# A decoder layer's first score stage: two score buffers instead of one, and the weights' low parts on another engine

## The reference, cut to what matters

```
x = layernorm(x + attn(x))        # linear attention, 16 heads of 16, causal, rms-normed values, output projection
x = layernorm(x + conv_mix(x))    # products of channel pairs with a context, long convolution, skip term
x = layernorm(x + ffn(x))         # gated network, width 2048, weights packed in 4-bit codes with scales
```

## Time and profile before

| | |
|---|---|
| three runs | 579.39 to 581.28 us, median 580.69 us |
| the profiled execution | 580.05 us, of which the span 578.4 us |
| TensorE matmul busy | 524.9 us (91% of the span) |
| VectorE busy | 375.6 us (65%), 782 instructions |
| ScalarE busy | 148.2 us (26%) |
| GpSimd busy | 123.5 us (21%), 195 instructions |
| granted TensorE clock, mean | 0.944 of full speed |

### The profile page before, as it was taken

The page is one execution under the profiler, slowest core; times in us unless marked ns, Lnnn a source line. Parts: engine busy times, 40 slices in busy tenths (PEclk is TensorE's granted clock), DMA queues, the critical chain, the costliest instruction groups (busy, mean ns, idle before and its releaser), DMA issues.

```text
span 578.4 us, 9097 instructions
## 1 busy us (share of the span) xinstructions
PE 524.9 (91%) x3280; PEld 428.4 (74%) x3280; DVE 375.6 (65%) x782; ACT 148.2 (26%) x259; POOL 123.5 (21%) x195
## 2 busy tenths in 40 slices
PE   5855569989989999999999999999999998599993
PEld 5722457776778888876788888776888887488883
DVE  3899659976768566886355577875455768733234
ACT  3422210153243211242232112232232110122220
POOL 2100038420001445030002445120003443200001
PEclk9965569999999999999999999999999999699998
DMA  5523214130020111005000110031001110100001
GB/s 164 160 79 73 71 53 132 56 95 16 21 72 23 43 37 47 0 29 156 1 1 28 47 47 28 0 88 57 0 0 44 47 54 1 37 1 0 1 1 37
DMA packets 25249, 26.69 MB, mean 46 GB/s; under 512 B 2816, under 2 KB 22784, under 8 KB 25216
## 3 DMA queue, kind: packets, MB, share of 16 engines
q1 hardware_dynamic: 14208, 15.73, 9.4%
q10 hardware_dynamic: 10576, 8.95, 5.2%
q0 software_dynamic: 432, 1.57, 0.8%
HBM read 24.15 MB, written 2.10 MB: 45 GB/s over the span
## 4 chain that ended last, share of the span: by engine, by line
PE 81%; DVE 11%; issue 3%; DMA 3%; POOL 1%; ACT 1%; ACTq 0%; POOLq 0%; DVEq 0%; SPq 0%
PE bank L903 16%; PE bank L905 15%; PE bank L904 15%; PE front_bank L1015 5%; PE front_bank L1018 4%; PE front_bank L1016 4%; PE front_bank L964 4%; PE front_bank L951 4%; PE front_bank L992 3%; PE front_bank L903 2%; PE front_bank L904 2%; PE front_bank L905 2%; DVE gate_q L676 2%; PE front_bank L974 1%; DMA wo_sb<-in_woT 1%
## 5 line engine op out<-in xcount | busy, mean ns | idle before, releaser
L903 PE MATMUL bank<-x2T_lo,ffn_hi 128*128 128x512 f32 x256 | 111.1, 434 | 4.1 <-DVE x2T_lo L838 4.1
L854 DVE TENSOR_TENSOR inter<-bank,inter 128x512 f32<-128x512 f32 x64 | 44.2, 690 | 94.3 <-PE bank L905 94.0
L905 PE MATMUL bank<-x2T_hi,ffn_hi 128*128 128x512 f32 x256 | 101.8, 397 | 0.0
L904 PE MATMUL bank<-x2T_hi,ffn_lo 128*128 128x512 f32 x256 | 101.4, 396 | 0.0
L436 POOL TENSOR_TENSOR qbd<-qT_sb,ctxT_sb 128x256 f32<-128x256 f32 x128 | 77.8, 631 | 77.5 <-PE front_bank L1018 63.8
L386 POOL TENSOR_TENSOR ve<-ve,minus_half 128x2 f32<-128x2 f32 x24 | 17.4, 743 | 305.5 <-DVE ve L726 235.4
L903 PE MATMUL bank<-ffn_lo,inter_hi 128*128 128x256 f32 x256 | 77.2, 302 | 0.8 <-DVE inter_lo L848 0.8
L588 ACT ACTIVATE inter_hi<-inter 128x512 fp32r<-128x512 f32 x64 | 40.5, 632 | 141.9 <-DVE inter L854 141.9
L582 ACT ACTIVATE inter<-bank 128x512 f32<-128x512 f32 x64 | 38.2, 598 | 134.3 <-PE bank L905 134.2
L905 PE MATMUL bank<-ffn_hi,inter_hi 128*128 128x256 f32 x256 | 72.0, 281 | 0.0
L904 PE MATMUL bank<-ffn_hi,inter_lo 128*128 128x256 f32 x256 | 71.9, 281 | 0.0
(11 more groups left out here) (113 smaller groups left out, 768.9 us busy)
## 6 DMA issues: line engine op xcount, KB each, us to landing
toep_sb<-in_toep ACTq DMA_DIRECT2D x64, 128.0 KB, 2.1
xT_sb<-in_xT SPq DMA_DIRECT2D x4, 512.0 KB, 6.1
ctxT_sb<-in_ctxT SPq DMA_DIRECT2D x4, 512.0 KB, 4.7
x_sb<-in_x SPq DMA_DIRECT2D x4, 512.0 KB, 5.7
ctx_sb<-in_ctx SPq DMA_DIRECT2D x4, 512.0 KB, 6.8
out<-ctxT_sb POOLq DMA_DIRECT2D x3, 512.0 KB, 3.4
raw_w<-in_gate_p SPq DMA_DIRECT2D x8, 128.0 KB
raw_s<-in_gate_s SPq DMA_DIRECT2D x8, 128.0 KB
```

Source lines behind the costliest of these rows:

```text
L854: nc.vector.tensor_tensor(inter[:, n % 2, :], up_ps[:, :], inter[:, n % 2, :], ALU.mult).then_inc(inter_ready, 1)
L903: nc.tensor.matmul(ps, w_hi, x_lo, start=start, stop=False, skip_group_check=True)
L904: nc.tensor.matmul(ps, w_lo, x_hi, start=False, stop=False, skip_group_check=True)
L905: return nc.tensor.matmul(ps, w_hi, x_hi, start=False, stop=stop, skip_group_check=True)
```

## The change

In the first group alone (`alone(g)`), odd score steps put their raw scores into the gated network's banks, now one tensor `ffn_ps` (`ffn_bank`), and their masked scores into `inter` (`odd_sc_sb`). TensorE's `score` there issues the raw scores of step u ahead of the values of step u-1; for u from 2 on they wait until mask step u-2 is done. VectorE's mask step waits for the values of step u-1 when u is even and of step u-2 when it is odd. And the low parts of all 24 units are computed by GpSimd, unit n directly after its high part, in place of VectorE two units later. In `turn`, GpSimd's first spread moves behind the first of its four pieces. The other groups' score steps keep their order.

```diff
+        odd_sc_sb = inter[:].rearrange("p n (h c) -> p (n h) c", c=P)
...
-        psum = [None] * 4 + [stack.enter_context(nc.psum_tensor(f"bank{i}", [P, T], F32)) for i in range(4, 8)]
+        ffn_ps = stack.enter_context(nc.psum_tensor("ffn_bank", [P, 4, T], F32))
...
+        def scores_ps(g, u):
+            return ffn_ps if alone(g) and u % 2 else front_ps
+        def masked_scores(g, u):
+            return odd_sc_sb if alone(g) and u % 2 else sc_sb
...
@@ GpSimd
+            def unpack(step):
+                n = step - 1
+                if 0 <= n < NU:
+                    m, c = units[n]
+                    pool.wait_ge(whi_ready, n + 1)
+                    nc.gpsimd.tensor_tensor(ffn_lo[:, m, :, c * QC:(c + 1) * QC], weight[:, n % 2],
+                                            ffn_hi[:, m, :, c * QC:(c + 1) * QC].bitcast(F32), ALU.subtract)\
+                        .then_inc(wlo_ready, 1)
...
                 if g is not None:
-                    for pair in range(4):
+                    beside(0)
+                    spread(g, 1)
+                    for pair in range(1, 4):
                         beside(pair)
-                    spread(g, 1)
...
@@ VectorE
-                q = n - 2
-                if 0 <= q < NU:
-                    m, c = units[q]
-                    dve.wait_ge(whi_ready, q + 1)
-                    nc.vector.tensor_tensor(ffn_lo[:, m, :, c * QC:(c + 1) * QC], weight[:, q % 2],
-                                            ffn_hi[:, m, :, c * QC:(c + 1) * QC].bitcast(F32), ALU.subtract)\
-                        .then_inc(wlo_ready, 1)
...
-                count(dve, o_mm, NU_S, g, u)
-                nc.vector.tensor_tensor(sc_sb.rearrange("p (r k) c -> p r k c", k=2),
-                                        front_ps[:, :, 0:2 * P].rearrange("p r (k c) -> p r k c", c=P),
+                count(dve, o_mm, NU_S, g, u - u % 2 if alone(g) else u)
+                nc.vector.tensor_tensor(masked_scores(g, u).rearrange("p (r k) c -> p r k c", k=2),
+                                        scores_ps(g, u)[:, :, 0:2 * P].rearrange("p r (k c) -> p r k c", c=P),
...
@@ TensorE
+            def raw_scores(g, u):
...
+                if alone(g) and u >= 2:
+                    count(pe, sm_ready, NU_S, g, u - 1)
...
             def score(g, u):
+                if alone(g):
+                    if u < NU_S:
+                        raw_scores(g, u)
+                    if u:
+                        values(g, u - 1)
+                else:
+                    if u:
+                        values(g, u - 1)
+                    if u < NU_S:
+                        raw_scores(g, u)
```

More of the change, by code:

```diff
@@ L140, in by_seq, with alone @@
             return tile[:, mt, :].rearrange("p (b t) -> p b t", t=S)
-        gate_ps, up_ps = psum[4], psum[5]
-        down_ps = psum[6:8]
-        skip_ps = x2T_ps = psum[4:6]
+        gate_ps, up_ps = ffn_ps[:, 0, :], ffn_ps[:, 1, :]
+        down_ps = [ffn_ps[:, i, :] for i in (2, 3)]
+        skip_ps = x2T_ps = [gate_ps, up_ps]
+        def alone(g):
+            return isinstance(g, int) and g == 0
+        def scores_ps(g, u):
+            return ffn_ps if alone(g) and u % 2 else front_ps
+        def masked_scores(g, u):
+            return odd_sc_sb if alone(g) and u % 2 else sc_sb
         def sems(*names):
@@ L449, in turn @@
                     pool.dma_start(out_v[:, bass.ds(at, NB), :], res_sb).then_inc(stored, 16)
-            schedule(pool, turn, {"score": score, "norm": norm, "x1T": x1T, "conv": conv}, nothing, nothing, nothing, nothing,
+            schedule(pool, turn, {"score": score, "norm": norm, "x1T": x1T, "conv": conv}, nothing, nothing, nothing, unpack,
                      lambda: rstd(G - 1, 2))
@@ L573, in turn @@
                         count(act, x2T_mm, 2, prev, w + 1)
[L574 removed]
+                        nc.scalar.activation(x2T_hi[:, w, :], x2T_ps[w], ACT.Copy).then_inc(x2hi_ready, 1)
                 if g is not None:
@@ L775, in x2_half @@
                 count(dve, skip_mm, 2, g, j + 1)
-                nc.vector.tensor_tensor(ctx2, skip_ps[j][:, :], ctx2, ALU.mult).then_inc(sk_ready, 1)
+                nc.vector.tensor_tensor(ctx2, skip_ps[j], ctx2, ALU.mult).then_inc(sk_ready, 1)
                 count(dve, cT_mm, 2, g, j + 1)
@@ L861, in finish @@
                     dve.wait_ge(last_mm, j + 1)
-                    nc.vector.tensor_tensor(res_sb[:, pair].rearrange("p b f -> p (b f)"), down_ps[j][:, :],
+                    nc.vector.tensor_tensor(res_sb[:, pair].rearrange("p b f -> p (b f)"), down_ps[j],
                                             x2_sb[:, pair].rearrange("p b f -> p (b f)"), ALU.add)\
@@ L938, in vproj @@
                 last.then_inc(v_mm, 1)
-            def score(g, u):
[L943 to L967, removed]
@@ new lines, in values @@
+            def values(g, v):
+                mt, b = v // NB, v % NB
+                if v == 0:
+                    count(pe, v_ready, 2, g, 2)
+                count(pe, sm_ready, NU_S, g, v + 1)
+                for odd in range(2):
+                    for pair in range(4):
+                        last = nc.tensor.matmul(
+                            front_ps[32 * pair:32 * pair + 32, b, 256 + mt * S:256 + (mt + 1) * S],
+                            v_sb[:, b, 4 * mt + pair, DK * odd:DK * odd + 2 * DK],
+                            masked_scores(g, v)[:, 2 * pair + odd, :], start=odd == 0, stop=odd == 1)
+                last.then_inc(o_mm, 1)
@@ new lines, in raw_scores @@
+            def raw_scores(g, u):
+                mt, b = u // NB, u % NB
+                if u == 0:
+                    count(pe, qk_ready, 4, g, 4)
+                    count(pe, v_ready, 2, g, 2)
+                if alone(g) and u >= 2:
+                    count(pe, sm_ready, NU_S, g, u - 1)
+                count(pe, spread_ready[u % 2], NU_S // 2, g, u // 2 + 1)
+                for r in range(4):
+                    rows = slice(32 * r, 32 * r + 32)
+                    last = nc.tensor.matmul(scores_ps(g, u)[:, r, 0:2 * P].rearrange("p (k c) -> p k c", c=P),
+                                            kT_sb[rows, mt, b * S:(b + 1) * S], q_two[rows, u % 4, 0:2],
+                                            start=True, stop=True)
+                last.then_inc(s_mm, 1)
```

10 lines of the change are left out of this document (5 added, 5 removed).

## The result

| | before | after |
|---|---|---|
| median of 12 runs each | 579.97 us (579.39 to 581.75) | 586.62 us (583.3 to 587.66) |
| ratio, 95% interval | | 1.0104 (1.0088 to 1.012) |
| the profiled execution; its span | 580.05; 578.4 us | 587.31; 585.7 us |
| VectorE busy | 375.6 us, 782 instructions | 379.7 us, 758 instructions |
| GpSimd busy | 123.5 us, 195 | 153.2 us, 219 |

The account below looks back on a forecast made before the run. A three-engine ring set the 3.59 us score step; breaking it would be waited away behind GpSimd's subtractions (3.66). Terms 0.8 + 2.2 + 0.7 + 0.3 + 0.5 = +4.5 on 580.05, plus 0.64 to the median: 585.2 us, range 581.5 to 588.5.

Parts of the forecast that it names:

- the rival of the races: Transposes, second `turn` and slot 6 at their low ends, first mask step at +0.2: +1.6, 582.2 us; chance 0.10.
- Start of the stage, +0.8: Up to the first mask step: GpSimd's subtractions delay unit 1 and meet pieces 2 and 4; +0.8 us, between -0.5 and +1.2.
- Score steps, +2.2: First group's steps 0 to 7: 3.66 us each plus 1.4 for three spreads, 27.0 against 24.84 us: +2.2.
- First layer norm, +0.7: Unit 15's subtraction delays the third and fourth normalisations and the last two transposes: +0.7 us, between 0 and +1.1.
- Second `turn`, +0.3: Unit 17's subtraction races the fourth normalisation: +0.9 - 0.48, or about -0.3 if the subtraction comes behind; taken as +0.3 us.
- Slot 6, +0.5: First group's back half: the subtraction starts beside VectorE's piece while TensorE idles; +1.0 - 0.48 gives +0.5 us, at best -0.5.
- The other slots: Other subtractions priced at nothing, lying where VectorE or GpSimd waits for TensorE; without that cover each could cost 0.5 us.
- The rival "no exclusion": GpSimd's subtraction does not keep VectorE out: step 2.79 us, -6.3 us in all, 574.4 us; chance 0.08.
- Slower GpSimd, 588: Rounding to float32r and two separate stretches make the subtraction 0.3 us slower in some ten places: 588 us; chance 0.12.
- An early release: The lock is let go after 0.47 us: score step 3.0 us, -2.4, the rest about even, 578.2 us; chance 0.06.

Follow-up runs that it names:

- e2: The changed kernel without its score part: one score buffer in the old order, low parts still on GpSimd; 586.40 us.
- e5: The changed kernel, but from piece 18 on (second `turn`, slots) GpSimd's subtraction also waits until VectorE's piece there is done; 582.65 us.
- e6: The changed kernel, but GpSimd subtracts unit 15 ahead of the first layer norm's powers instead of behind them; 585.64 us.
- e1: The changed kernel without its GpSimd part: two score buffers, low parts on VectorE again; 578.47 us.
- e3: The changed kernel with the first twelve pieces' and piece-18-on subtractions waiting for VectorE, unit 15 before the first layer norm's powers, unit 16 behind the second's normalisations; 575.24 us.
- e7: The changed kernel, but in the first twelve pieces GpSimd's subtraction also waits until VectorE's next unit is done; 580.87 us.
- e9: The kernel with all subtractions moved, and the first group's odd spreads on ScalarE instead of GpSimd; 574.63 us.
- e8: The changed kernel with each GpSimd subtraction replaced by a memset of zeros of the same size; 575.93 us.

## Why the prediction was right, and where it was not

The forecast, 585.2 us and slower, lies 1.4 us below the measured 586.62. That it lies so near is in part luck: it stood on 580.69, the median of three runs, where twelve give 579.97, so that the change cost 6.65 us and the forecast of +4.5 is 2.15 short. (One small slip: the rival of the races comes to 580.69 + 1.6 = 582.3, not 582.2.) Its reason held: GpSimd's subtraction and the instructions of VectorE that the sum named, shifts, bit mask, product and normalisations, exclude each other for their whole length. The mark that it gave for them, to read and write SBUF alone, is too wide, as the last section shows. The row on which it rested, and that no trace of before had, is the pair of 42.77: it waits until 43.72 for an instruction of 512 columns. The Trainium skill, "SBUF — State Buffer", section "Who interferes with whom", has the lock held for the full instruction; the trace agrees for the subtraction, with 1.27 us. Step by step:

- **Start of the stage, +0.8:** +0.84, beside a -0.56 of earlier transfers that has nothing to do with the change (that event lies at 13.56 to 14.72 us in the ten traces). The prediction had pieces 2 and 4 meet a subtraction. All of pieces 1 to 4 did, and idle time took up the rest; the size is right, the account of it too small. The size also holds beyond the one trace: it is 16.04 to 16.38 us in the four kernels with this front (after, e2, e5, e6), and 15.30 and 15.54 in the two without the subtractions (e1, before).
- **Score steps, +2.2:** +1.75. A step is 3.62, not 3.66, since the subtraction starts 0.74 us behind a piece's end (38.41 - 37.67) and not 0.79; a spread behind it costs 0.42 (1.73 - 1.31), not 0.47, three times.
- **First layer norm, +0.7:** +0.83. The third and fourth normalisations waited for unit 15's subtraction. e6 took it away and got 0.77 back at that place. The 0.31 us in the convolution were not in the sum: TensorE's clock was 0.50 from 86 to 92 us, where it was 0.95 before. Whether they belong to the change is not shown: e1, without the subtractions, takes 27.54 us for that stretch, as against 27.27 before and 27.58 after.
- **Second `turn`, +0.3:** +0.63. The prediction left open which side wins the race, and took a value between. The subtraction won, twice. VectorE, then GpSimd of the kernel after, in order of time:

```profile
124.99 1.58 DVE L671 SCALAR_TENSOR_TENSOR weight<-code,raw_s 128x512 f32<-128x512 f16 x1
126.50 2.33 DVE L754 TENSOR_SCALAR x_sb<-x_sb,mv,ve 128x256 f32<-128x256 f32 x4
...
124.56 1.47 POOL L457 TENSOR_TENSOR ffn_lo<-weight,ffn_hi 128x512 fp32r<-128x512 f32 x1
127.32 1.36 POOL L457 TENSOR_TENSOR ffn_lo<-weight,ffn_hi 128x512 fp32r<-128x512 f32 x1 [1.29 <-ACT ffn_hi L510]
```

  Unit 16's subtraction holds up the product with the scales (1.58 us), unit 17's the normalisations (2.33 instead of 1.37). The prediction had seen the second one alone.
- **Slot 6, +0.5:** +0.64, as described, by a subtraction that started 0.02 us ahead of the shifts.
- **What was missing:** the +1.56 behind slot 6, a term that the sum had at nothing without a reason. The prediction priced TensorE's longer idle time at its length and stopped there; it did not ask what the clock does behind a longer gap. e5 shows both go together: without the gap neither is there. The other slots were rightly priced at nothing (0 and -0.21 us over their stretches).

The five terms of the sum came to 4.7 us where 4.5 stood. What moves the time beyond it is the clock: behind slot 6 by the longer gap (e5), at the convolution (0.31) and at the end of the kernel (1.42 us of the profiled run) without a cause that a run shows. The rival "no exclusion", 574.4 us, is refuted as a mechanism, and its time came true another way: e3, in which the exclusion is there but falls mostly on work that it does not touch, takes 575.24. Slower GpSimd, 588, did not happen where the two did not meet: 1.27 us, as the earlier trace rows, so rounding to float32r costs it nothing. An early release is refuted by the stretched pair.

Two things stay open. Two of the twelve runs of the changed kernel took 583.3 and 583.5 us at a mean clock of 0.944 to 0.947, and the others 585.4 to 587.7 at 0.934 to 0.940; which stretch of low clock those two were spared no trace shows. Where slot 6 has the same gap, other kernels have such runs too (one of four of e2 at 583.1, three of ten of e7 at 577.6 to 578.8 against 580.5 to 582.5), so it is not shown that the 1.56 us, seen in four traces of four, falls due in every run. And nothing was tried against the transfer that ends the wait in e9.

## What to carry to other kernels

Work handed from VectorE to GpSimd was free here while VectorE waited or ran its mask step, which has an input in PSUM; over the shifts, masks, products and normalisations, which read and write SBUF alone, it cost VectorE GpSimd's longer time (1.27 us here) for VectorE's shorter one (0.69). So look not at how idle GpSimd is, but at which of VectorE's instructions its own will fall on, and put it there by a wait: a few added waits for a later event made the same instructions 1% faster than before instead of 1% slower. And where TensorE idles already, price a longer gap by the clock behind it as well.

## What the runs showed of the hardware that was not expected

- An instruction of GpSimd that reads nothing holds VectorE's shifts too: the zeros of e8, until 40.23, against a pair that starts at 40.03 and takes 0.54 us instead of 0.48; of the overlap the first 0.14 us cost nothing, as in the other pairs here (0.12 to 0.14). The mask step, with one input in PSUM, is not touched: 1.22 us under a subtraction (e7) as without one (e1).
- Not every instruction that reads and writes SBUF alone is held. In the kernel after, all 64 reductions of the convolution (`TENSOR_REDUCE`) take 0.69 us, though 43 of them lie for 0.3 us and more beside GpSimd's products, and the first of two `BATCH_NORM_STATS2` keeps its 0.43 us wholly under a subtraction. Nor does every instruction of GpSimd hold VectorE: two normalisations keep 0.41 us each under the power of 81.87 to 82.70. The line of the reductions over all (ns min/median/max, first and last start, forms), then VectorE and GpSimd in order of time:

```profile
L786 DVE TENSOR_REDUCE gate_q<-qbd x64: 685/686/689, 90.3 to 492.3; 128x64 f32<-128x512 f32 x64
...
186.50 0.75 DVE L737 BATCH_NORM_STATS2 st<-x_sb 128x6 f32<-128x256 f32 x2
...
185.76 1.30 POOL L457 TENSOR_TENSOR ffn_lo<-weight,ffn_hi 128x512 fp32r<-128x512 f32 x1 [3.96 <-ACT ffn_hi L510]
```

- The clock fell behind 2.18 us of idle TensorE in four kernels (0.64 to 0.69 over the next 4 us in after, e2, e6, e7) and stayed at 1.00 behind 1.53 (before), 1.52 (e1) and 1.06 us (e5). In these traces 0.65 us more of idling cost 1.56 us more behind it.
- The clock comes back at different times at the same place of the program: the 16 products of the first output projection took 5.32 us in e1, 5.80 in e6, 6.00 in e2, and 6.31 to 6.71 in the other kernels.
